# Gated-edges stage of a graph network: a third buffer of gathered rows, GpSimd three steps ahead, a VectorE loop of six steps

## The reference

```python
src, dst = (edge_index[0], edge_index[1])
concat = jnp.concatenate([h[src], h[dst], edge_attr], axis=-1)
gates = jax.nn.sigmoid(concat @ W_e + b_e)
messages = jax.nn.softplus(concat @ W_n + b_n)
gated = gates * messages
h_new = jax.ops.segment_sum(gated, dst, num_segments=n)
edge_count = jnp.clip(segment_sum(ones, dst), 1.0, None)[:, None]
return h + h_new / edge_count
```

## Time and profile before

| | |
|---|---|
| median of 3 runs | 3197.06 us |
| the profiled execution: span | 3184.9 us |
| `gated_edges`: first gather to last add | 1276.5 to 2551.5 us (its start) |
| granted TensorE clock in that stage | 0.50 |
| busy in the whole span | PE 84%, DVE 53%, ACT 43%, POOL 28% |

### The profile page before, as it was taken

The page is one execution under the profiler, slowest core; times in us unless marked ns, Lnnn a source line. Parts: engine busy times, 40 slices in busy tenths (PEclk is TensorE's granted clock), DMA queues, the critical chain, the costliest instruction groups (busy, mean ns, idle before and its releaser), DMA issues. The chain is left out here.

```text
span 3184.9 us, 66445 instructions
## 1 busy us (share of the span) xinstructions
PE 2666.3 (84%) x21196; PEld 2393.9 (75%) x21197; DVE 1691.5 (53%) x3605; ACT 1361.4 (43%) x2809; POOL 905.6 (28%) x1144
## 2 busy tenths in 40 slices
PE   3888889869999998788878888888878769859999
PEld 2777778759999996666666666666666657649999
DVE  7877787773444436544444444444444452355555
ACT  2444444423333334344444444444444431207776
POOL 2111211200000000566655666566656600000000
PEclk7999999979999998555555555555555559878999
DMA  2333333320000002444434444443434360028272
GB/s 68 115 101 100 104 115 102 103 76 2 2 2 2 2 2 75 121 107 103 103 101 102 106 103 103 101 106 102 104 101 103 101 243 24 1 88 348 92 260 78
DMA packets 221040, 300.38 MB, mean 94 GB/s; under 512 B 101187, under 2 KB 186662, under 8 KB 215430
## 3 DMA queue, kind: packets, MB, share of 16 engines
q1 hardware_dynamic: 181926, 217.20, 21.6%
q0 software_dynamic: 38880, 79.68, 10.3%
HBM read 225.96 MB, written 70.80 MB: 93 GB/s over the span
## 5 line engine op out<-in xcount | busy, mean ns | idle before, releaser
L1130 POOL DMA_INDIRECT layer_R<-source_terms,layer_srcs x804 | 764.0, 950 | 500.0 <-DVE layer_zp L1174 275.5
L1332 PE MATMUL layer_zp<-layer_Wa,layer_at 64*128 64x192 f32 x1620 | 606.7, 538 | 244.4 <-issue 242.5
L1332 PEld LDWEIGHTS layer_zp<-layer_Wa,layer_at 64*128 64x128 f32 x1620 | 488.1, 322 | 308.4 <-issue 301.4
L536 PE MATMUL build_win<-nodes_x,build_S 128*128 128x200 bf16 x5264 | 501.4, 253 | 125.2 <-DVE nodes_x L453 117.2
L536 PEld LDWEIGHTS build_win<-nodes_x,build_S 128*128 128x128 bf16 x5264 | 442.7, 99 | 180.1 <-DVE nodes_x L453 116.8
L931 PE MATMUL layer_acc<-layer_U,graph_CT 128*128 128x192 f16 x6250 | 521.4, 247 | 19.0 <-DVEq L761 19.0
L931 PEld LDWEIGHTS layer_acc<-layer_U,graph_CT 128*128 128x128 f16 x6250 | 517.3, 98 | 26.5 <-issue 22.7
L1174 DVE TENSOR_TENSOR layer_zp<-layer_zp,layer_R 128x1152 f32<-128x1152 f32 x135 | 183.7, 1361 | 399.4 <-remote 399.4
L1282 ACT ACTIVATE layer_y<-layer_zp 128x1152 f32<-128x1152 f32 x135 | 152.6, 1130 | 472.7 <-DVE layer_zp L1174 439.9
L1356 PEld LDWEIGHTS layer_acc<-layer_hot,layer_G 128*98 128x98 f32 x1644 | 287.3, 288 | 38.0 <-issue 35.5
L1356 PE MATMUL layer_acc<-layer_hot,layer_G 128*98 128x32 f32 x1644 | 292.6, 349 | 15.1 <-DVE layer_G L1186 5.0
(11 more groups left out here) (243 smaller groups left out, 2873.9 us busy)
## 6 DMA issues: line engine op xcount, KB each, us to landing
layer_ring<-W_blocks SPq DMA_DIRECT2D x41, 1600.0 KB, 7.7
W_blocks<-nodes_x SPq DMA_DIRECT2D x400, 100.0 KB, 1.8
layer_at<-in_attr SPq DMA_DIRECT2D x135, 192.0 KB
C_blocks<-build_Cblk SPq DMA_DIRECT2D x25, 800.0 KB, 3.5
layer_C<-C_blocks SPq DMA_DIRECT2D x25, 800.0 KB, 21.4
layer_rows<-target_rows SPq DMA_DIRECT2D x135, 144.0 KB
layer_R<-source_terms,layer_srcs POOLq DMA_INDIRECT x804
layer_Qs<-target_terms SPq DMA_DIRECT2D x135, 36.0 KB
```

The costliest lines, as they stand in the source:

```text
L536: mm = pe.matmul(out, S[:, b, part, 2 * i + u, :, :].rearrange("p a z -> p (a z)"), M[:, i, u, :, :].rearrange("p a z -> p (a z)"), start= ...
L1130: nc.gpsimd.indirect_dma_start(R[:, h, u, :], None, P_d, bass.IndirectOffsetOnAxis(ap=at_u, axis=0)).then_inc(s_R[h], 16)
L1332: mm = pe.matmul(out[u], at[:, h, u * P:(u + 1) * P], Wa[:, :], start=(u % 2 == 0), stop=False, skip_group_check=True)
```

## The change

The buffer of gathered rows gets three parts (`RB = 3`), with a semaphore each; step s uses part r = s % 3. GpSimd waits, from step 3 on, for the add of three steps before; the first three steps wait for no add. VectorE's loop holds `ROUND` = 6 steps, so that both s % 2 and s % 3 are fixed within it: 22 turns, and three steps behind it. To make room for the third semaphore, the `edge_ranges` stage loads two inputs on one semaphore.

```diff
+RB = 3
+ROUND = 2 * RB
@@ edge_ranges
-        s_in = [m.sem(f"edges_loaded{i}") for i in range(4)]
+        s_in = [m.sem(f"edges_loaded{i}") for i in range(3)]
-            sp.dma_start(dstI[:, :], dst_cols[:, 0:ETB]).then_inc(s_in[2], 16)
+            sp.dma_start(dstI[:, :], dst_cols[:, 0:ETB]).then_inc(s_in[1], 16)
-            dve.wait_ge(s_in[1], 16)
-            dve.wait_ge(s_in[2], 16)
+            dve.wait_ge(s_in[1], 32)
@@ gated_edges
-        R = m.sb("R", [P, 2, SE, D2], F32)
+        R = m.sb("R", [P, RB, SE, D2], F32)
-        s_R = [m.sem(f"source_terms_gathered{h}") for h in range(2)]
+        s_R = [m.sem(f"source_terms_gathered{r}") for r in range(RB)]
             for s in range(NS):
-                h = s % 2
+                r = s % RB
                 if s == 1:
                     pool.wait_ge(s_srcs, 16)
-                pool.wait_ge(s_add, s + 1)
+                if s >= RB:
+                    pool.wait_ge(s_add, s - RB + 3)
...
-            def add(h, s, turn):
-                dve.wait_ge(s_R[h], (turn * 16 + 16) * SE)
+            def add(h, r, s, third):
+                dve.wait_ge(s_R[r], (third * 16 + 16) * SE)
                 dve.wait_ge(s_z, s + 3)
-                nc.vector.tensor_tensor(zp[h][:, :, 0:D2], zp[h][:, :, 0:D2], R[:, h, :, :], ALU.add).then_inc(s_add, 1)
+                nc.vector.tensor_tensor(zp[h][:, :, 0:D2], zp[h][:, :, 0:D2], R[:, r, :, :], ALU.add).then_inc(s_add, 1)
...
-            with dve.Fori(0, NS // 2) as pair:
-                for h in range(2):
-                    step(h, pair * 2 + h, pair, False)
-            step(0, NS - 1, NS // 2, True)
+            with dve.Fori(0, NS // ROUND) as turns:
+                for i in range(ROUND):
+                    step(i % 2, i % RB, turns * ROUND + i, turns * RB + i // 2, turns * 2 + i // RB, False)
+            for s in range(NS // ROUND * ROUND, NS):
+                step(s % 2, s % RB, s, s // 2, s // RB, s == NS - 1)
```

More of the change, by code:

```diff
@@ L142, in _ @@
             sp.dma_start(srcI[:, :], src_cols[:, 0:ETB]).then_inc(s_in[1], 16)
-            sp.dma_start(dstI[:, :], dst_cols[:, 0:ETB]).then_inc(s_in[2], 16)
+            sp.dma_start(dstI[:, :], dst_cols[:, 0:ETB]).then_inc(s_in[1], 16)
             sp.wait_ge(s_made, 5)
-            sp.dma_start(weight[:, edges], w_cols[:, 0:ETB]).then_inc(s_in[3], 16)
+            sp.dma_start(weight[:, edges], w_cols[:, 0:ETB]).then_inc(s_in[2], 16)
             sp.wait_ge(s_r16, 1)
@@ L178, in twice @@
                 nc.scalar.activation(pair[:, a, :, :], column.unsqueeze(2).to_broadcast([P, ETK, 2]), ACT.Copy).then_inc(s_part, 1)
-            act.wait_ge(s_in[3], 16)
+            act.wait_ge(s_in[2], 16)
             twice(1, weight[:, :])
@@ L1130, in _ @@
                     nc.gpsimd.indirect_dma_start(
-                        R[:, h, u, :], None, P_d,
-                        bass.IndirectOffsetOnAxis(ap=at_u, axis=0)).then_inc(s_R[h], 16)
+                        R[:, r, u, :], None, P_d,
+                        bass.IndirectOffsetOnAxis(ap=at_u, axis=0)).then_inc(s_R[r], 16)
         @block.vector
@@ L1213, in accumulate, with step @@
                         dve.sem_inc(s_taken, 1)
-            def step(h, s, turn, last):
+            def step(h, r, s, turn, third, last):
                 gated(h, s - 2)
@@ L1220, in step @@
                 logs(1 - h, s - 1)
-                add(h, s, turn)
+                add(h, r, s, third)
                 if not last:
```

## The result

| | before | after |
| --- | --- | --- |
| median, us (14 runs each) | 3198.12 (3195.50 to 3200.24) | 3204.95 (3199.36 to 3208.08) |
| ratio after / before, 95% interval | | 1.0016 (1.0009 to 1.0023) |
| span of the profiled execution, us | 3184.9 | 3205.4 |
| first gather to first add, us | 18.60 | 25.76 |
| distance of adds, in turn, us | 6.29 / 12.56 | 6.29 / 12.68 |

The medians lie 6.8 us apart; the ratio, which compares runs made side by side, says 0.16%, 5.1 us (2.9 to 7.4). Predicted were 3199 us and most likely no difference. The spans alone would say 20 us, but the two profiled executions are not a pair. Where both are known, an execution's time is 1.8 to 2.5 us above its span (3207.21 and 3205.4 us for the kernel after). So the profiled execution of before, with its span of 3184.9 us, took about 3187 us, less than any of the 14 runs. The runs are the comparison.

A forecast was written before the change was run, and what follows sets the result against it. TensorE's signals, held up once per pair of steps, were taken to bound the kernel. 3184.9 + 0 + 2 + 0 + 0 = 3186.9 us, plus 12.2 us, gave 3199 us; range 3020 to 3267 us, the forecast's own 3193 to 3206.

The forecast's parts named there:

- What ends the stall: VectorE's even-step add: it waits for TensorE's late signal, 7.1 us after the matmuls' end, not for gathered rows.
- Part (1): Third buffer, GpSimd waiting three steps back: rows already came in time, so the steady state changes by 0.
- rival B: VectorE's loop: stalls hang on its branch back, 45 pairs lose theirs, 173 us go, 3024 us; chance 0.12.
- Part (2): Start of the stage: 18 gathers in a row instead of 12 may delay the first add; 0 to 6.5 us, 2 taken.
- (3): VectorE's loop of six steps: fewer branches, possible code loading of up to 70 us if uncovered; taken as 0.
- Part (4): The `edge_ranges` stage waits for two loads on one semaphore, as it waited for both before; 0.
- same: Whole kernel: a measured time of 3190.7 to 3203.5 us counts as no change; chance 0.53.
- The 12.2 us: Whole kernel: amount by which the median of the runs before stands above the profiled span, added to the sum.
- A: VectorE's add waits for the gather: stalls go, GpSimd's 7.5 us per step is next, 260 us faster, 2937 us; chance 0.08.
- C: VectorE's loop no longer stays loaded: 24 to 70 us slower, 3221 to 3267 us; chance 0.18 including like losses.
- D: GpSimd: steady runs of 18 gathers would lengthen each stall by 7.5 us; expected only at the start, no separate chance.

The follow-up runs named there:

- Experiment 3: Kernel before with no gathers from the third step on, later source terms left out: 2886.04 us, ratio 0.906.
- 4: Kernel before with three gathers per step instead of six, the other three tiles without source terms: 2883.58 us, ratio 0.905.
- 5: Kernel before with GpSimd's gathers replaced by plain copies of fixed rows from the third step on, same bytes and number: 2879.76 us, ratio 0.900.
- 6: Kernel before with six plain copies of fixed rows per step issued by SyncE, GpSimd issuing nothing: 2881.24 us, ratio 0.900.
- 7: Kernel before with six iotas per step on GpSimd in place of the gathers from the third step on: 2939.78 us, ratio 0.918.
- 9: Kernel before with fourteen plain copies per step by GpSimd (six of 98 KB, eight of 24 KB) in place of the gathers: 2983.35 us, ratio 0.931.
- experiment 12: Kernel before with six gathers per step reading rows 0 to 127 in order from the third step on: 3196.11 us against 3196.88, ratio 1.000.
- experiment 2: Kernel after with the third step's gathers again waiting for the first add, so its first run stops after 12 gathers: 3194.08 us, ratio 1.0022.
- experiment 1: Kernel before with only VectorE's loop of six steps, two buffers kept: 3188.14 us against 3187.86, ratio 1.000.
- experiment 10: Kernel before with five gathers per step instead of six, one tile without source terms: 3186.55 us, ratio 0.994.

## Why the prediction was right, and where a size was off

**What ends the stall.** The prediction read a TensorE signal, held during GpSimd's run, out of the earlier trace rows. Right: L1175 passes 7.6 us ahead of the add again. Its suspicion of the gathers, for which no row gave a cause, is now shown by leaving them out (experiments 3 and 4), and narrowed to their indexed form (5, 6, 7, 9, 12).

**Part (1), steady state, price 0.** Right in the price. The kernel after alone would suggest 66 x 0.12 = 8 us, but on one chip three buffers and two have the same long distance, 12.545 and 12.546 us (experiments 2 and 1). The runs of 12 gathers and the four microseconds between them were forecast and are there. One sentence of this part is wrong: with TensorE's signals in time the gather would soon be late, as a pair would want 12.58 us and GpSimd needs 15.0, which rival B reckons with. Experiment 3 puts TensorE's own pace at 14.2 us per pair, still under 15.0. So the stall hides a second limit 0.4 us per step behind it, which the buffer wouldn't lift either.

**Part (2), the start.** This is the term that was mis-sized. I worked out an upper bound of 6.5 us and took 2, "since the first run before already had 12 gathers and its add was not late". It is 25.76 - 18.60 = 7.16 us, just over the bound, since the add came 3.0 us behind the run and not 2.4. With it the sum would have been 3204 us; 3204.95 was measured. That is 1.4 us above the prediction's own upper end of "same", 3203.5; the ratio, 5.1 us, lies within its 6.4. So "same" came out, but closely, and not thanks to the 2 us that I took. The argument for 2 was the weak one: 12 gathers just didn't reach the first add, 18 did. Experiment 2 shows that the loss belongs to the surplus run and not to the start: it is paid wherever GpSimd first gets ahead by a buffer.

**Parts (3) and (4), price 0.** Right for the loop by experiment 1. The kernel after, DMA queues, window 1360 to 2500:

```profile
q8 instruction: 1, 0.02, 0.0%
```

This is the whole of that queue in 1140 us, one packet at 1363.1, the fourth of the stage; the kernel before has its fourth at 1352.7, just ahead of the window of the earlier trace rows. No packet comes back with the 22 turns of the loop. By the Trainium skill, page "Runtime: NRT & Kernel Launch", section "Instruction fetch mechanics", a taken branch to code outside the two loaded blocks would first load it. The trace shows no such load for a loop of 228 instruction rows on VectorE, and experiment 1 no cost. Part (4) had no run of its own.

**The 12.2 us.** The sum added them as the distance of median and span. They are not that (1.8 us in the kernel after): the profiled execution of before was faster than any of the 14 runs. The addition was right all the same, since it brings the sum back to the median of the runs.

**The rivals.** A (the gather is waited for): refuted by L1175, and nothing of its 260 us is in the time. B (one stall per turn of VectorE's loop): refuted by the 66 stalls of experiment 1. C (loop's code): refuted by the same run. D (longer runs hold TensorE longer): true for the one run of 18, 7.2 us there and 8.5 us in experiment 2, and absent after it.

**Open.** What in an indexed transfer holds TensorE, and where. Signals are raised late although their matmuls have ended, as far as the profile's modelled ends tell, and matmuls without a wait start late too. Runs of ten or more gathers hold TensorE and runs of three don't, but whether the length of the run, GpSimd's share or the pause behind it decides wasn't settled: five per step (83% of the gathers) are held like six, three with 0.58 us between are held less, three with 3.65 us between are not.

## What to carry to other kernels

A deeper buffer helps only if the data is what comes last. Look for the queue instruction that carries the data's wait: if it passes microseconds ahead of the work (here 7.6 us), more buffers only let the producer run longer in one piece, and here that piece itself cost 7 us. Where signals of one engine arrive in a bunch long after its work, see which other engine goes idle just before the bunch, and leave its work out in one run: 6 gathers to 0 and to 3 told more than any rearrangement of waits. And when a shorter hold wins nothing, look whether the wait has moved to an earlier place of the same engine's step, as from the add to `accumulate` in experiment 10.

## What was not expected of the hardware

- GpSimd's indexed transfers of 128 rows (0.95 us each, 0.30 us apart), in runs of ten or more, delay TensorE's semaphore signals mostly by 5 to 9 us, and by up to 15.8 us in the run of 18 of experiment 2, until 2 to 3.4 us after the run's end (with 12 gathers 2.4 us), and make its matmuls start in steps of some 0.7 us (starts at 2018.77, 2020.18, 2020.91 in experiment 12; 2022.65, 2024.76, 2026.15 in the kernel after). Without half of the gathers 300 us of 3190 go here; of them some 250 us are the hold's by my estimate, since with all gathers GpSimd's pace of 7.5 us per step would be the limit in place of 9.38 on average (134 x 1.9 us). Plain copies by GpSimd (0.54 us each, without a gap between) don't do it at any density tried, nor at a higher DMA share (0.61 against 0.41).
- The effect is not proportional: three gathers per step cost nothing (ratio 0.905, as with none), five as good as the full price (0.994).
- Where TensorE is held, records of its semaphores are missing in the trace: of 97 `s_z` 16 in the kernel before, of 95 with five gathers 47. A lateness that is read to the next record of the same semaphore comes out far too long there (16 us for signals that VectorE had used 3.4 us after the matmul).
